# The product of state and C in two selective scans, moved to VectorE with C read from PSUM

## The chip, the cores and the metric

The kernel runs on one core of a Trainium2 chip. The metric is the device time of one execution in microseconds (us). Five engines work from queues of their own, each in order, and wait for one another by semaphores: TensorE (PE; its weight loads are shown as PEld), VectorE (DVE), ScalarE (ACT), GpSimd (POOL) and SyncE (SP), which here only issues DMAs.

## What is computed

The program is a decoder of four layers with three blocks each, on 16 sequences of 128 positions and 256 features. Two of the twelve blocks are selective state-space scans: the attention slot of layer 1 (512 inner channels) and that of layer 3 (256 channels). The change touches these two alone. The one of layer 3, cut to its core:

```python
A = jnp.exp(A_log)
Bm = h @ w_B.T + b_B                      # 16 states per position
Cm = h @ w_C.T + b_C
Delta = jax.nn.softplus((h @ w_d1.T + b_d1) @ w_d2.T + b_d2)
A_bar = jnp.exp(-Delta[..., None] * A)
BX = (Delta * h)[..., None] * Bm[:, :, None, :]
_, states = jax.lax.associative_scan(comb, (A_bar, BX), axis=1)
y = jnp.einsum('blfn,bln->blf', states, Cm) + D * h
```

The block of layer 1 computes the same recurrence from other projections.

## The kernel before

The twelve blocks run one after the other as stages, with a barrier of all engines between them. Channels lie on the 128 partitions, positions along the free dimension. The 16 sequences are taken in four groups of four, so a group has 4 x 128 = 512 columns (GT).

Both scan blocks share the class `Scan`. It works in units: one unit is a group and 256 channels, two slabs of 128, hence tiles of 128 x 2 x 512. The mamba stage (layer 1, 512 channels) has eight units, the sequence_ssm stage (layer 3) has four; I number them from 0 in each stage. A unit has 16 steps, one for each state n, 192 steps in all. A step n consists of

- "spread" n. TensorE multiplies a selecting matrix with the rows of B and C (L1156), which copies row n of B to all partitions in PSUM bank 4 and row n of C in bank 5. There are these two banks alone, so the spread of n+1 into a bank has to wait until the reader of n is done with it. ScalarE takes the exponentials into `decay` (L1173, two) and copies C's bank into the SBUF tile `ccol` (L1178). VectorE multiplies dt*x with B's bank into `drive` (L1188).
- "scan" n. VectorE runs the recurrence along the positions (L1196), from `decay` and `drive` into `state`. GpSimd then multiplies `state` in place with `ccol` (L1203).
- "sum" n. TensorE adds `state` to the unit's y in PSUM with an identity matrix (L1162): two matmuls in fp32, which the records show as four passes of 512 columns.

There are two tiles of decay, three of drive and three of state.

The order is written out by hand in `Scan.steps`. Every engine walks the same list and does its own part of each entry. Between the entries of a step stand two slots, a and b, each for one piece of other work: first what is left of the unit before ("finish", "out" and the like), then the preparation of the next group ("stats", "apply", "turn", "inner", "conv", "project", "split", "delta", "step" and others). A step reads: spread n+1, slot a, scan n, sum n-2, slot b. When a unit's pieces are used up, its steps are clean: only scan work is in them. At the end of a unit come sums 14 and 15, and behind them spread 0 of the next unit.

`Fills` counts how often a set of PSUM banks has been filled and emptied; its last argument names the engine that empties each bank in turn ("va": bank B by VectorE, bank C by ScalarE). The pieces that both stages put into the slots use two more banks, `side`.

## Time and profile before

| | us |
|---|---|
| median of 3 runs | 5046.37 |
| lowest, highest | 5042.47, 5047.23 |
| the profiled execution | 5043.2 |
| its span, first to last instruction | 5041.9 |

| engine | busy us | share of the span |
|---|---|---|
| TensorE | 3389.6 | 67% |
| VectorE | 2613.4 | 52% |
| ScalarE | 1957.9 | 39% |
| GpSimd | 1435.7 | 28% |

The shares are means over twelve stages that differ in what limits them, so they don't tell what the two scan stages wait for. In the timeline a row is one instruction or several merged ones of one engine and line; its columns are the start in us, the length in us, the engine, the line, the operation, the names written and read with their shapes, and how many instructions the row merges. In brackets stands the time for which the engine waited in front of it and what released it. An engine that starts an instruction before the record of the one ahead has ended shows starts closer together than the lengths; so steps are read from start to start. The granted clock of TensorE has two levels, full (2.4 GHz, 1.0) and half (1.2 GHz, 0.5), and a stretch shows its mean.

### The profile page before, as it was taken

How to read it: one execution, taken by the hardware profiler on the slowest of the kernel's cores; microseconds unless marked ns; L12 is line 12 of the kernel's file. 1: busy time of each engine (PE TensorE's matmuls, PEld its weight loads, DVE VectorE, ACT ScalarE, POOL GpSimd, SP SyncE). 2: the span in 40 equal slices, each digit the busy share in tenths (PEclk: the TensorE clock that was granted, in tenths of full speed). 3: DMA queues.
4: the chain of work that ended last, by engine and by line, in shares of the span. 5: the costliest groups of instructions: out<-in, count | busy, mean ns of one | idle time of the engine just before them, and what ended most of it. 6: DMA issues, size and time to landing. Idle time of an engine off the chain costs nothing. (4 is left out here: it accounts for less than half of the span.)

```text
span 5041.9 us, 52801 instructions
## 1 busy us (share of the span) xinstructions
PE 3389.6 (67%) x17501; PEld 2163.4 (43%) x17501; DVE 2613.4 (52%) x6543; ACT 1957.9 (39%) x3879; POOL 1435.7 (28%) x1085
## 2 busy tenths in 40 slices
PE   2666666638695366666668888856759766666688
PEld 1445544535463122222246656634546522224555
DVE  3555555534633488778933323354543257674443
ACT  2777777721121343443323333322412243433411
POOL 1444444421144334334411111120001134440010
PEclk8888888868898678777889999978968878788889
DMA  3000000012044100000000000011021200000000
GB/s 78 1 1 1 1 1 1 1 46 100 20 126 119 64 0 0 0 0 0 0 13 7 1 1 1 1 33 69 1 84 35 51 21 0 0 0 24 1 1 17
DMA packets 70666, 116.10 MB, mean 23 GB/s; under 512 B 28321, under 2 KB 58169, under 8 KB 67650
## 3 DMA queue, kind: packets, MB, share of 16 engines
q1 hardware_dynamic: 60802, 86.49, 5.4%
q0 software_dynamic: 9600, 26.23, 2.1%
q8 instruction: 148, 2.42, 0.2%
q14 instruction: 116, 0.95, 0.1%
HBM read 88.58 MB, written 24.12 MB: 22 GB/s over the span
## 5 line engine op out<-in xcount | busy, mean ns | idle before, releaser
L1203 POOL TENSOR_TENSOR L_attn_state<-L_attn_state,L_attn_ccol 128x1024 f32<-128x1024 f32 x192 | 481.1, 2509 | 678.7 <-DVE L_attn_state L1196 678.7
L1196 DVE TENSOR_TENSOR_SCAN L_attn_state<-L_attn_decay,L_attn_drive 128x1024 f32<-128x1024 f32 x192 | 583.1, 3042 | 0.2
L1162 PE MATMUL bank<-L_attn_state,ident 128*128 128x512 f32 x768 | 476.7, 757 | 60.4 <-POOL L_attn_state L1203 60.4
L1173 ACT ACTIVATE L_attn_decay<-L_attn_dt,L_attn_A 128x512 f32<-128x512 f32 x384 | 256.3, 715 | 344.2 <-DVE L_attn_state L1196 342.6
L1156 PE MATMUL bank<-L_attn_parts,L_attn_select 96*128 96x512 bf16 x384 | 158.4, 454 | 292.5 <-DVE L_attn_drive L1188 160.8
L1162 PEld LDWEIGHTS bank<-L_attn_state,ident 128*128 128x128 f32 x768 | 181.8, 242 | 259.9 <-issue 159.6
L1188 DVE TENSOR_TENSOR L_attn_drive<-L_attn_dtx,bank 128x1024 f32<-128x1024 f32 x192 | 230.4, 1200 | 111.3 <-PE bank L1156 111.2
L1083 POOL TENSOR_TENSOR L_xattn_prob<-L_xattn_prob,L_xattn_inv 128x1024 f32<-128x1024 f32 x64 | 121.3, 1895 | 570.9 <-DVE L_xattn_inv L1066 570.9
L1156 PEld LDWEIGHTS bank<-L_attn_parts,L_attn_select 96*128 96x128 bf16 x384 | 37.1, 106 | 479.6 <-DVE L_attn_drive L1188 260.7
L1178 ACT COPY L_attn_ccol<-bank 128x512 f32<-128x512 f32 x192 | 112.2, 585 | 295.2 <-POOL L_attn_state L1203 179.5
L716 ACT ACTIVATE L_xattn_prob<-bank,L_xattn_top 128x128 f32<-128x128 f32 x512 | 135.8, 416 | 197.1 <-DVE L_xattn_top L758 197.1
L2729 POOL TENSOR_TENSOR L_attn_t<-L_attn_t 128x512 f32<-128x512 f32 x96 | 121.7, 1268 | 305.5 <-ACT L_attn_t L2542 305.4
L1007 ACT ACTIVATE L_xattn_prob<-L_xattn_masked,L_xattn_low 128x256 f32<-128x256 f32 x256 | 126.9, 496 | 210.0 <-DVE L_xattn_low L1061 121.9
L2725 POOL TENSOR_TENSOR L_attn_t<-L_attn_t,L_attn_base 128x1024 f32<-128x1024 f32 x96 | 183.2, 1908 | 62.1 <-DVE L_attn_base L2675 62.1
L2698 DVE RECIPROCAL L_attn_den<-L_attn_den 128x512 f32<-128x512 f32 x32 | 107.3, 3353 | 139.4 <-ACT L_attn_den L2580 139.4
L1061 DVE CUSTOM_DVE_ANT_0 L_xattn_masked<-bank,L_xattn_hidden 128x256 f32<-128x256 f32 x256 | 93.3, 421 | 130.9 <-PE bank L921 130.9
L898 PE MATMUL bank<-L_xattn_kvT,L_xattn_wk 128*128 128x256 f32 x512 | 127.6, 392 | 37.2 <-ACT L_xattn_kT L963 19.6
L2679 DVE MATCH_REPLACE8 L_attn_t<-L_attn_top,L_attn_t 128x64 f32<-128x64 f32 x768 | 150.3, 207 | 0.0
L907 PE MATMUL bank<-L_xattn_wv,L_xattn_kvT 128*128 128x512 f32 x256 | 127.0, 618 | 28.6 <-ACT L_xattn_v L971 16.7
L2491 PE MATMUL bank<-L_attn_sm,L_attn_fv 128*64 128x128 f32 x512 | 50.0, 357 | 122.1 <-issue 122.1
L3379 POOL DMA_INDIRECT L_ffn_xh<-L_ffn_rows,L_ffn_tokens x96 | 91.2, 950 | 136.5 <-PE bank L3186 77.4
L2440 PE MATMUL bank<-L_attn_kbd,L_attn_qT 128*128 128x512 f32 x192 | 125.3, 743 | 0.0
(605 smaller groups left out, 8271.0 us busy)
## 6 DMA issues: line engine op xcount, KB each, us to landing
L_ffn_ew<-in_L_ffn_experts SPq DMA_DIRECT2D x4, 3072.0 KB, 20.0
L_ffn_made<-L_ffn_yout SPq DMA_DIRECT2D x24, 512.0 KB, 3.0
L_ffn_w<-in_L_ffn_w SPq DMA_DIRECT2D x4, 2048.0 KB, 14.6
L_xattn_ctx<-in_ctx_rows SPq DMA_DIRECT2D x3, 2048.0 KB, 8.3
L_ffn_rows<-L_ffn_xh SPq DMA_DIRECT2D x8, 512.0 KB, 3.0
L_ffn_made<-L_ffn_yout SPq DMA_DIRECT2D x12, 256.0 KB, 2.1
X<-in_x SPq DMA_DIRECT2D x16, 128.0 KB
turned<-X SPq DMA_DIRECT2D x16, 128.0 KB
```

The costliest lines, as they stand in the source:

```text
L716: t = act.activation(prob[n % 2][j][:, i, :], score[j].bank(n)[:, i * P:(i + 1) * P], ACT.Exp, bias=top[:, j, i:i + 1])
L898: t = pe.matmul(side.bank(at)[:, i * 2 * P:(i + 1) * 2 * P], w["wk"][:, k, col:col + P], kvT[a % 2][:, k, :], start=k == 0, stop=k == KC - 1)
L907: t = pe.matmul(side.bank(at)[:, :], kvT[a % 2][:, k, half * P:(half + 1) * P], w["wv"][:, k, cols], start=k == 0, stop=k == KC - 1)
L1007: t = act.activation(prob[n % 3][:, h, :], masked[n % 2][:, h, :], ACT.Exp, bias=low[:, n % 2, h:h + 1], scale=-1.0, accum_out=total[:, n ...
L1156: pe.matmul(self.spread.bank(2 * N + i)[:, :], self.select[:, NSTATE * i + n, :], parts[:, :], start=True, stop=True).then_inc(*self.sprea ...
L1162: t = pe.matmul(self.y[unit % len(self.y)][m][:, :], self.c.ident[:, :], self.state[N % 3][:, m, :], start=n == 0, stop=n == 15)
L1173: t = act.activation(self.decay[N % 2][:, m, :], dt[:, m, :], ACT.Exp, scale=A[:, m, n:n + 1])
L1188: dve.tensor_tensor(self.drive[N % 3][:, :, :], dtx[:, :, :], self.spread.bank(2 * N)[:, :].unsqueeze(1).broadcast_to([P, 2, GT]), ALU.mul ...
L1196: dve.tensor_tensor_scan(flat(self.state[N % 3]), flat(self.decay[N % 2]), flat(self.drive[N % 3]), 0.0, ALU.mult, ALU.add).then_inc(*self ...
L1203: pool.tensor_tensor(state[:, :, :], state[:, :, :], self.ccol[N % 2][:, :].unsqueeze(1).broadcast_to([P, 2, GT]), ALU.mult).then_inc(*sel ...
L2679: m = dve.match_replace(t[n % RING][:, 1, i, :], top[n % 2][:, i, :], t[n % RING][:, 0, i, :], -1e30)
L2725: pool.tensor_tensor(both, both, base[n % 2][:, :].unsqueeze(1).unsqueeze(3).broadcast_to([P, 2, per, nkeys]), ALU.subtract).then_inc(*shi ...
```

## The change

ScalarE's copy of C (`ccol`) and GpSimd's product are taken out. VectorE does the product right behind the scan, in place on `state`, with the second operand read from C's PSUM bank. It first waits for C's spread and for its own scan, and its end marks C's bank as empty and the state as ready for the sum. In `steps` the spread of n+1 moves from ahead of slot a to behind the scan of n: a step now reads slot a, scan n, spread n+1, sum n-2, slot b.

```diff
-        self.spread = Fills(s, "spread", banks, "va")
+        self.spread = Fills(s, "spread", banks, "v")
...
         yield "spread", 16 * unit
         for n in range(16 * unit, 16 * unit + 16):
+            yield from one()
+            yield "scan", n
             if n % 16 != 15:
                 yield "spread", n + 1
-            yield from one()
-            yield "scan", n
             if n % 16 >= 2:
                 yield "sum", n - 2
             yield from one()
...
-            pe.wait_ge(*self.weighted.at(N))
+            pe.wait_ge(*self.spread.emptied(2 * N + 1))
...
-            if N >= 2:
-                act.wait_ge(*self.weighted.at(N - 2))
-            act.wait_ge(*self.spread.filled(2 * N + 1))
-            act.copy(self.ccol[N % 2][:, :], self.spread.bank(2 * N + 1)[:, :]).then_inc(*self.spread.done(2 * N + 1))
...
-    def gpsimd(self, what, N):
-        if what == "scan":
-            pool, state = self.c.nc.gpsimd, self.state[N % 3]
-            pool.wait_ge(*self.spread.emptied(2 * N + 1))
-            pool.wait_ge(*self.scanned.at(N))
-            pool.tensor_tensor(state[:, :, :], state[:, :, :], self.ccol[N % 2][:, :].unsqueeze(1).broadcast_to([P, 2, GT]), ALU.mult).then_inc(*self.weighted.up())
+            state = self.state[N % 3]
+            dve.wait_ge(*self.spread.filled(2 * N + 1))
+            dve.wait_ge(*self.scanned.at(N))
+            dve.tensor_tensor(state[:, :, :], state[:, :, :], self.spread.bank(2 * N + 1)[:, :].unsqueeze(1).broadcast_to([P, 2, GT]), ALU.mult).then_inc(*self.spread.done(2 * N + 1))
```

The rest of the diff drops `ccol`, the flag `weighted` and the calls of `scan.gpsimd`. Lines behind it move up by a few, so L1188 and L1196 of before are L1184 and L1192 after, the product is L1196 after, and the convolution of the sequence_ssm stage, L1546 before, is L1537.

VectorE in the sequence_ssm stage, unit 1, steps 5 to 7, before. Names are the tiles written and read; the scan is listed as SCALAR_TENSOR_TENSOR, L1655 is the piece "inner" and L1661 begins the piece "normal":

```order
L1196 SCALAR_TENSOR_TENSOR L_attn_state_35170<-L_attn_decay_35166,L_attn_drive_35167 128x1024
L1655 TENSOR_SCALAR L_attn_h_35139<-bank,L_attn_cols 128x4x128
L1188 TENSOR_TENSOR L_attn_drive_35169<-L_attn_dtx_35147,bank 128x1024
L1655 TENSOR_SCALAR L_attn_h_35139<-bank,L_attn_cols 128x4x128
L1196 SCALAR_TENSOR_TENSOR L_attn_state_35171<-L_attn_decay_35165,L_attn_drive_35168 128x1024
L1188 TENSOR_TENSOR L_attn_drive_35167<-L_attn_dtx_35147,bank 128x1024
L1196 SCALAR_TENSOR_TENSOR L_attn_state_35172<-L_attn_decay_35166,L_attn_drive_35169 128x1024
L1661 BN_STATS L_attn_cbn_35153<-bank 128x6 x4
```

And after, the same place:

```order
L1192 SCALAR_TENSOR_TENSOR L_attn_state_34786<-L_attn_decay_34782,L_attn_drive_34783 128x1024
L1196 TENSOR_TENSOR L_attn_state_34786<-L_attn_state_34786,bank 128x1024
L1184 TENSOR_TENSOR L_attn_drive_34784<-L_attn_dtx_34763,bank 128x1024
L1646 TENSOR_SCALAR L_attn_h_34755<-bank,L_attn_cols 128x4x128 x2
L1192 SCALAR_TENSOR_TENSOR L_attn_state_34787<-L_attn_decay_34781,L_attn_drive_34784 128x1024
L1196 TENSOR_TENSOR L_attn_state_34787<-L_attn_state_34787,bank 128x1024
L1184 TENSOR_TENSOR L_attn_drive_34785<-L_attn_dtx_34763,bank 128x1024
L1192 SCALAR_TENSOR_TENSOR L_attn_state_34788<-L_attn_decay_34782,L_attn_drive_34785 128x1024
L1196 TENSOR_TENSOR L_attn_state_34788<-L_attn_state_34788,bank 128x1024
L1184 TENSOR_TENSOR L_attn_drive_34783<-L_attn_dtx_34763,bank 128x1024
L1652 BN_STATS L_attn_cbn_34769<-bank 128x6 x4
```

Scan, product and drive now follow one another, a drive is the one for the very next scan, and the pieces of slot b and of the next slot a stand together.

TensorE at the same place before (L1533 is "turn", L1539 "inner", L1546 "conv"):

```order
L1533 MATMUL bank<-ident,L_attn_xn 128x128 x4
L1162 MATMUL bank<-L_attn_state_35171,ident 128x512 x2
L1539 MATMUL bank<-L_attn_xT,L_attn_w_in 128x512 x2
L1156 MATMUL bank<-L_attn_parts_35149,L_attn_select_35164 128x512 x2
L1539 MATMUL bank<-L_attn_xT,L_attn_w_in 128x512 x2
L1162 MATMUL bank<-L_attn_state_35172,ident 128x512 x2
L1546 MATMUL bank<-L_attn_h_35139,L_attn_w_conv 128x512 x6
L1156 MATMUL bank<-L_attn_parts_35149,L_attn_select_35164 128x512 x2
L1546 MATMUL bank<-L_attn_h_35139,L_attn_w_conv 128x512 x6
L1162 MATMUL bank<-L_attn_state_35170,ident 128x512 x2
```

And after:

```order
L1524 MATMUL bank<-ident,L_attn_xn 128x128 x8
L1156 MATMUL bank<-L_attn_parts_34765,L_attn_select_34780 128x512 x2
L1162 MATMUL bank<-L_attn_state_34787,ident 128x512 x2
L1530 MATMUL bank<-L_attn_xT,L_attn_w_in 128x512 x4
L1156 MATMUL bank<-L_attn_parts_34765,L_attn_select_34780 128x512 x2
L1162 MATMUL bank<-L_attn_state_34788,ident 128x512 x2
L1537 MATMUL bank<-L_attn_h_34755,L_attn_w_conv 128x512 x12
L1156 MATMUL bank<-L_attn_parts_34765,L_attn_select_34780 128x512 x2
L1162 MATMUL bank<-L_attn_state_34786,ident 128x512 x2
```

Spread and sum stand together in front of the two pieces, where a piece stood between them; the two convolutions are one block of twelve matmuls behind the spread.

## Rows read from the trace of the kernel before

**Rows 1.** Costliest groups: line, engine, names, count | busy us, mean ns | idle before.

```profile
L1203 POOL TENSOR_TENSOR L_attn_state<-L_attn_state,L_attn_ccol 128x1024 f32<-128x1024 f32 x192 | 481.1, 2509 | 678.7 <-DVE L_attn_state L1196 678.7
L1196 DVE TENSOR_TENSOR_SCAN L_attn_state<-L_attn_decay,L_attn_drive 128x1024 f32<-128x1024 f32 x192 | 583.1, 3042 | 0.2
```

**Rows 2.** Timeline of clean steps, mamba unit 3, all engines.

```profile
2079.43 2.28 DVE L1196 TENSOR_TENSOR_SCAN L_attn_state<-L_attn_decay,L_attn_drive 128x1024 f32<-128x1024 f32 x1
2081.64 1.20 DVE L1188 TENSOR_TENSOR L_attn_drive<-L_attn_dtx,bank 128x1024 f32<-128x1024 f32 x1
...
2081.86 2.35 POOL L1203 TENSOR_TENSOR L_attn_state<-L_attn_state,L_attn_ccol 128x1024 f32<-128x1024 f32 x1 [12.64 <-DVE L_attn_state L1196]
2082.75 3.61 DVE L1196 TENSOR_TENSOR_SCAN L_attn_state<-L_attn_decay,L_attn_drive 128x1024 f32<-128x1024 f32 x1
...
2086.28 1.19 DVE L1188 TENSOR_TENSOR L_attn_drive<-L_attn_dtx,bank 128x1024 f32<-128x1024 f32 x1
...
2087.40 3.61 DVE L1196 TENSOR_TENSOR_SCAN L_attn_state<-L_attn_decay,L_attn_drive 128x1024 f32<-128x1024 f32 x1
```

**Rows 3.** Timeline at the end of mamba unit 2, all engines.

```profile
2058.99 5.79 DVE L1196 TENSOR_TENSOR_SCAN L_attn_state<-L_attn_decay,L_attn_drive 128x1024 f32<-128x1024 f32 x2
...
2062.75 6.47 POOL L1203 TENSOR_TENSOR L_attn_state<-L_attn_state,L_attn_ccol 128x1024 f32<-128x1024 f32 x2 [2.29 <-DVE L_attn_state L1196]
...
2066.97 6.55 PE L1162 MATMUL bank<-L_attn_state,ident 128*128 128x512 f32 x8 [3.51 <-POOL L_attn_state L1203]
...
2073.88 1.22 DVE L1188 TENSOR_TENSOR L_attn_drive<-L_attn_dtx,bank 128x1024 f32<-128x1024 f32 x1 [9.09 <-PE bank L1156]
...
2076.79 1.40 DVE L1418 SCALAR_TENSOR_TENSOR L_attn_xc<-L_attn_xc,L_attn_cols,bank 128x512 f32<-128x512 f32 x2
```

**Rows 4.** Timeline, mamba unit 2, VectorE: scans 0, 8 and 12.

```profile
1947.73 2.28 DVE L1196 TENSOR_TENSOR_SCAN L_attn_state<-L_attn_decay,L_attn_drive 128x1024 f32<-128x1024 f32 x1
...
2010.68 2.28 DVE L1196 TENSOR_TENSOR_SCAN L_attn_state<-L_attn_decay,L_attn_drive 128x1024 f32<-128x1024 f32 x1
...
2051.02 2.29 DVE L1196 TENSOR_TENSOR_SCAN L_attn_state<-L_attn_decay,L_attn_drive 128x1024 f32<-128x1024 f32 x1
```

**Rows 5.** Timeline, sequence_ssm unit 1, VectorE: scans 0, 2, 3, 6, 8, 12, next 0.

```profile
4202.78 2.28 DVE L1196 TENSOR_TENSOR_SCAN L_attn_state<-L_attn_decay,L_attn_drive 128x1024 f32<-128x1024 f32 x1
...
4214.34 2.28 DVE L1196 TENSOR_TENSOR_SCAN L_attn_state<-L_attn_decay,L_attn_drive 128x1024 f32<-128x1024 f32 x1
...
4220.16 2.26 DVE L1196 TENSOR_TENSOR_SCAN L_attn_state<-L_attn_decay,L_attn_drive 128x1024 f32<-128x1024 f32 x1
...
4249.57 2.28 DVE L1196 TENSOR_TENSOR_SCAN L_attn_state<-L_attn_decay,L_attn_drive 128x1024 f32<-128x1024 f32 x1
...
4262.82 2.28 DVE L1196 TENSOR_TENSOR_SCAN L_attn_state<-L_attn_decay,L_attn_drive 128x1024 f32<-128x1024 f32 x1
...
4296.80 2.28 DVE L1196 TENSOR_TENSOR_SCAN L_attn_state<-L_attn_decay,L_attn_drive 128x1024 f32<-128x1024 f32 x1
...
4325.30 2.28 DVE L1196 TENSOR_TENSOR_SCAN L_attn_state<-L_attn_decay,L_attn_drive 128x1024 f32<-128x1024 f32 x1
```

**Rows 6.** Timeline, VectorE: an instruction that waits for the one before it.

```profile
1729.65 1.22 DVE L1404 TENSOR_TENSOR L_attn_dt<-L_attn_dt,L_attn_soft 128x1024 f32<-128x1024 f32 x1 [10.11 <-ACT L_attn_soft L1358]
1730.91 1.23 DVE L1407 TENSOR_TENSOR L_attn_dtx<-L_attn_dt,L_attn_xc 128x1024 f32<-128x1024 f32 x1
```

**Rows 7.** Timeline, sequence_ssm unit 1, steps 5 and 6, ScalarE and TensorE.

```profile
4238.42 0.59 ACT L1178 COPY L_attn_ccol<-bank 128x512 f32<-128x512 f32 x1 [5.05 <-POOL L_attn_state L1203]
...
4244.66 1.88 PE L1162 MATMUL bank<-L_attn_state,ident 128*128 128x512 f32 x4
...
4246.37 2.74 PE L1546 MATMUL bank<-L_attn_h,L_attn_w_conv 128*128 128x512 f32 x6
```

**Rows 8.** Busy time by window: us, each engine (count), granted clock, DMA share, GB/s.

```profile
4200.00:4325.00 125.00, 79.89 (x174) 32.95 (x174) 85.05 (x97) 52.40 (x78) 54.13 (x32) 0.80 0.00 0
```

**Rows 9.** One line's instructions: count, ns min/median/max, first and last start, forms.

```profile
L1390 DVE SCALAR_TENSOR_TENSOR L_attn_xc<-L_attn_xi,L_attn_cols,L_attn_xc x48: 750/752/2724, 1695.6 to 2223.7; 128x512 f32<-128x512 f32 x48
```

More of the change, by code:

```diff
@@ L1104, in __init__ @@
         self.decay, self.drive = [s.sb(f"decay{n}", [P, 2, GT]) for n in range(2)], [s.sb(f"drive{n}", [P, 2, GT]) for n in range(3)]
-        self.state, self.ccol = [s.sb(f"state{n}", [P, 2, GT]) for n in range(3)], [s.sb(f"ccol{n}", [P, GT]) for n in range(2)]
+        self.state = [s.sb(f"state{n}", [P, 2, GT]) for n in range(3)]
         self.mid, self.rest = s.sb("mid", [2 * NSTATE, GT], BF16), s.sb("rest", [2 * NSTATE, GT])
-        self.spread = Fills(s, "spread", banks, "va")
+        self.spread = Fills(s, "spread", banks, "v")
         self.y = [ybanks[2 * n:2 * n + 2] for n in range(len(ybanks) // 2)]
-        self.decayed, self.scanned, self.weighted, self.summed = (s.flag(n) for n in ("decayed", "scanned", "weighted", "summed"))
+        self.decayed, self.scanned, self.summed = (s.flag(n) for n in ("decayed", "scanned", "summed"))
         self.selected, self.split_up, self.parted = s.flag("selected"), s.flag("split_up", 4), s.flag("parted")
@@ L1455, in gpsimd @@
             pool.tensor_tensor(rs, rs, power[:, :], ALU.mult).then_inc(*norm.inverse.up())
-        elif what == "scan":
-            scan.gpsimd(what, n)
     return Part(order, tensor, scalar, vector, gpsimd)
@@ L1771, in gpsimd @@
             last.root(n)
-        elif what == "scan":
-            scan.gpsimd(what, n)
     return Part(order, tensor, scalar, vector, gpsimd)
```

## The prediction

> **What bounds the kernel now.** I read the list of costliest groups first. Its two top rows are a pair: GpSimd's product of state and C (L1203) and VectorE's scan (L1196), 192 of each [rows 1]. Both scan stages ("mamba" and "sequence_ssm") are VectorE's. The timeline of a stretch with no side work shows it [rows 2]: a scan starts at 2082.75, the next multiply into drive at 2086.28, the next scan at 2087.40, so a step is 4.65 us and VectorE never stops. The reader is to see one more thing there. The scan at 2079.43, which comes after a pause of GpSimd, takes 2.28; the later ones take 3.61, because GpSimd's product (2.35, started at 2081.86) still runs when they are due and holds them until it ends at 2084.21. So a clean step costs 1.11 + 2.20 (both start to start) and 1.33 of being held.
>
> Two other kinds of time lie in these stages. At the end of each unit of 16 steps VectorE waits for TensorE: GpSimd needs 6.47 us for the last two products, TensorE's last eight summing passes start only at 2066.97, the next unit's spread comes behind them, and drive starts at 2073.88, after 9.09 us of waiting [rows 3]; there are 12 such ends. And where the next group's preparation is woven in (units 0, 2, 4 of the first stage, all but the last of the second), VectorE often waits for a piece's matmuls. One unit of each stage stands in rows by its scans [rows 4, 5].
>
> **The change, part by part.** *GpSimd's product and ScalarE's copy go.* With no GpSimd work beside it a scan is 2.28 again, worth 1.33 in each of some 110 held ones (583.1 - 192 x 2.28 = 145 us, and 145 / 1.33 = 109) [rows 1, 2]. ScalarE's copy lies beside other work; nothing on VectorE waits for it in a clean step.
>
> *VectorE gets 192 products*, of 128x1024 with one PSUM operand, the form of drive (1.20) [rows 2]. The product reads what the scan just wrote, and now each drive stands right in front of its scan, so two starts a step wait for VectorE's own last result. Such a pair stands in [rows 6]: 1.22 long, next start after 1.26, so 0.04 after the end, where an unbound next one starts 0.08 before it (1.19 to 1.11). A clean step becomes 2.28 + 0.04, 1.22 - 0.08, 1.19 + 0.04 = 4.69 us: 0.04 longer than before. Bounds: 4.62 if the bound starts cost nothing, 4.85 if all three pay 0.1. The Trainium skill ("VectorE: DVE Perf Modes", the section on the TRN2 errata) gives a PSUM source 120 fixed cycles and an SBUF source 58, some 0.065 us more for each product; by it the sum would be 12 us higher. The rows speak against it: drive with a PSUM operand takes 1.20, the pair with two SBUF operands 1.22 and 1.23 [rows 6].
>
> *The unit's end.* Let T be the start of scan 15. Product 14 ended at T - 1.15. Behind it TensorE has C's spread, the sums 12, 13, 14, 15 (four passes each) and the next B's spread: about 18 passes. A pass is 0.43 at the full clock (a sum of four starts at 4244.66, the work behind it 1.71 later) and twice that, 0.86, at the half one [rows 7]; with a granted clock of 0.80 over a unit, 0.6 of the time is full and a mean pass is 0.54 [rows 8]. So drive 16 starts at T - 1.1 + 18 x 0.54 = T + 8.6 (T + 6.7 all full, T + 13.7 all half); before it was T + 11.3 (scans 14 and 15 take 5.79 from 2058.99, so T is 2062.53). Then drive 1.14 and finish 2.64 (two L1418, one L1422, read from 2076.79 to 2079.43): 12.4 from scan to scan, against 16.9. A clean unit is thus 15 x 4.69 + 12.4 = 82.8 where 83.0 stood: nothing. The gain at the end pays for a drive that used to be done before the unit began.
>
> *The spread on TensorE, the part that decides.* C(n+1) goes into the bank that C(n) leaves, and TensorE's queue is in order. Before, ScalarE's copy emptied that bank early, so TensorE ran ahead: at 4244.66 it did a sum and from 4246.37 the first conv passes, while the scan on VectorE only began at 4249.57 [rows 5, 7]. Now that bank is free only at P, the end of product n. Queued behind this wait are C(n+1), sum n-2, the piece of slot b and the piece of the next slot a; ScalarE's copies and VectorE's own pieces wait for these. TensorE reaches slot b at P + 0.1 + 0.45 + 2.15 = P + 2.7, VectorE is there at P + 1.15. The order also joins slots b and a, with scan, product and drive all on the other side.
>
> I walk the sequence unit from 4202.78 to 4325.30 [rows 5], scan to scan, now and then:
> - scans 0 to 2 (back, last, out): 11.6, then 15.0. back starts after product 0 (3.45) instead of beside scan 0.
> - 2 to 3 (out, stats): 5.8, then 11.2: 3.45 + 2.7 + 2.5 passes' time of out, 0.95 for its add, 1.7 for stats.
> - 3 to 6 (whole, apply, turn, inner): 29.4, then 26.8. ScalarE's copy of C, held 5.05 us by GpSimd at 4238.42 with the copy of xT behind it, is gone [rows 7].
> - 6 to 8 (conv, normal, [rows 7]): 13.3, then 21.6: 3.45 + 2.7, both convs as one block of 24 passes at the full clock 10.4, spread 0.4, and then drive 1.15 and twice 1.7 of normal. Scan 7 and its product hide in it.
> - 8 to 12 (silu, project, rank, split, delta, step): 34.0, then 43.5. project starts 1.6 later, rank and delta each start 2.7 behind a product, and the chain through ScalarE starts that much later.
> - 12 to the next unit: 28.5, then 3 x 4.69 + 12.4 = 26.5.
>
> Sum 122.5, then 144.6: +22. The next unit is the same at 120.9 (+24), the first has no finish pieces (+13), the last has them and nothing more, and ends a little sooner (+9): +68 for this stage.
>
> The same walk for the mamba unit from 1947.73 to 2079.43 [rows 2, 4]: scans 0 to 8 (out, stats, apply, four convs that are VectorE's own) 62.9, then 66.8, all of it in the out and apply pieces; 8 to 12 (silu, project, delta, split, step) 40.3, then 47.6, of which project and delta, held as above, are 3.5 and 3.8; the rest 28.4, then 26.5. Sum 131.7, then 140.9: +9. Unit 4 is the same work in 129.0, +12. Unit 0, where stats and apply now have scan, product and drive between them, -1; the five others together 0. First stage: +20.
>
> **Sum.** The profiled execution took 5043.2 (span 5041.9 and 1.3 around it), 3.2 below the median of 5046.4. 5043.2 + 20 + 68 = 5131; against the median I forecast **5134 us**. The unknown that moves it most is TensorE's pass: all mixed segments at 0.43 would give about 35 us back, all at 0.86 would add about 50.
>
> **Rivals.**
> - *The products hide, chance 0.09, 5010 us (faster).* Of the 125 us around the unit of [rows 5] VectorE is busy 85 [rows 8], so some 30 us of waits lie in its mixed steps. If every product there falls into a wait that some other chain sets (GpSimd's root, ScalarE's tables), the mixed segments keep their times. Then eight mixed units gain 2 us each (end less tail), and the pieces that GpSimd holds behind a scan get shorter: eight of the 48 of L1390 from 2.72 to 0.75 [rows 9], 16 us, with some 4 of others: -36. For it: the stretch 3 to 6 above, where ScalarE's queue was the cause. Against it: TensorE's in-order wait on the product, which lengthens just the chains that VectorE waits for. It decides if TensorE gets to slot b less than 1.15 after P. Near it stands the Trainium skill ("SBUF — State Buffer", "Who interferes with whom"): of a VectorE instruction with two SBUF inputs and a GpSimd one that reads SBUF, the second is blocked whole; by that rule the 145 us of held scans come back.
> - *Halves of both, chance 0.05, 5046:* full clock throughout the mixed segments and half of their products hidden.
> - *TensorE mostly at its half clock in the held segments, chance 0.10, 5184:* it now stands still before each block, and eight passes after a pause took 6.55 us [rows 3], nearly all at the half clock.
> - *The hold isn't GpSimd's, chance 0.03, 5280:* if 3.61 stays, 110 steps of 6.0 add 150 us. Against it: the one scan of 2.28 [rows 2], with the same operands, and GpSimd's end at 2084.21 plus 2.2 is the scan's end.
>
> **How the numbers follow.** Forecast 0.73 with 5090 to 5175 as its own range. The range of 8 in 10 goes from 5075 to 5182. A measurement of this kernel tells about 0.2% (10 us) from no change. Slower by more: 0.73 + 0.10 + 0.03 and a little of the mixed case, 0.87; within: 0.04; faster: 0.09.
>
> **What would show it.** Right: scans all near 2.28; clean steps at 4.65 to 4.75; idle of VectorE before drive or before normal of about 9 us at the convs of the sequence stage, released by TensorE; TensorE's spread released by VectorE's product, with the sum and the piece starting behind it; drive of a new unit 8 to 9 us after scan 15 starts. Wrong: convs of the sequence stage starting before product 6 ends, unchanged segments 6 to 8 and 8 to 12, or clean steps off 4.69 by more than 0.1, each tenth of which is worth 11 us.

## The result, and the profile after

| | before | after |
|---|---|---|
| median of 4 runs, us | 5046.8 | 5411.06 |
| lowest, highest | 5042.47, 5049.84 | 5406.45, 5415.06 |
| span of the profiled execution | 5041.9 | 5407.8 |
| ratio, 95% interval | | 1.0722, 1.0704 to 1.0741 |

The change makes the kernel slower by 364 us. The forecast was slower by 88, in a range that ended at 5182. The direction was right and the size was wrong by a factor of four.

The scan's row among the costliest groups after, in the columns of [rows 1]:

```profile
L1192 DVE TENSOR_TENSOR_SCAN L_attn_state<-L_attn_decay,L_attn_drive 128x1024 f32<-128x1024 f32 x192 | 439.3, 2288 | 315.2 <-PE bank L1162 313.6
```

The scan was busy 583.1 us in [rows 1] and is busy 439.3 now: the 144 us in which GpSimd held it are back, as forecast. But in front of it stand 315 us of idle time, where the row of before had 0.2, and nearly all of that ended with TensorE's sum (L1162). VectorE's waits, listed by what ended them (us in total, times, longest), say it once more:

```profile
DVE L_attn_state L1192 <- PE bank L1162: 313.6, 118, 3.0
```

118 waits of at most 3.0 us are some 2.7 us each. The timeline of clean steps shows one of them (mamba unit 3, VectorE and TensorE; before: [rows 2]):

```profile
2197.98 2.29 DVE L1192 TENSOR_TENSOR_SCAN L_attn_state<-L_attn_decay,L_attn_drive 128x1024 f32<-128x1024 f32 x1 [2.98 <-PE bank L1162]
...
2200.38 1.22 DVE L1196 TENSOR_TENSOR L_attn_state<-L_attn_state,bank 128x1024 f32<-128x1024 f32 x1
2201.52 1.21 DVE L1184 TENSOR_TENSOR L_attn_drive<-L_attn_dtx,bank 128x1024 f32<-128x1024 f32 x1
...
2201.66 0.61 PE L1156 MATMUL bank<-L_attn_parts,L_attn_select 96*128 96x512 bf16 x1 [3.29 <-DVE L_attn_state L1196]
...
2202.06 3.62 PE L1162 MATMUL bank<-L_attn_state,ident 128*128 128x512 f32 x4
...
2205.47 0.63 PE L1156 MATMUL bank<-L_attn_parts,L_attn_select 96*128 96x512 bf16 x1
2205.72 2.29 DVE L1192 TENSOR_TENSOR_SCAN L_attn_state<-L_attn_decay,L_attn_drive 128x1024 f32<-128x1024 f32 x1 [2.99 <-PE bank L1162]
```

The reader is to follow a circle. The product ends at 2201.60. C's spread starts at 2201.66, when its bank is free, and the sum follows it at 2202.06. The sum ends at 2205.68 (2202.06 + 3.62), and the next scan starts at 2205.72. Then come scan and product, and it begins anew: 7.73 us a step, of which VectorE is busy 4.64. The scan waits for this sum because there are only three tiles of state: scan n writes the tile that sum n-3 reads (`summed.at(N - 3)`), and the sum that stands behind C(n) is sum n-3. The four passes take 3.62 at the half clock; elsewhere in the same unit a sum takes less and a step 7.0 to 7.5. Steps 0 and 1 of a clean unit take 4.88, since no sum stands behind their spreads yet. Of the 364 us, 212 lie in the first stage and 149 in the second (from its first scan to that of the second, and from there to the end of the program).

The windows of one clean unit and one with pieces (length; busy and count of PE, PEld, DVE, ACT, POOL; granted clock, DMA share, GB/s) show both stages: 83.0 us became 116.9 and 122.5 became 159.4, and the clock fell from 0.79 in both units to 0.68 and 0.70.

```profile
2143.76:2260.62 116.86, 62.29 (x96) 20.99 (x96) 76.84 (x52) 21.34 (x32) 0.00 (x0) 0.68 0.00 0
4449.12:4608.51 159.39, 91.32 (x174) 36.89 (x174) 94.46 (x110) 40.54 (x60) 13.00 (x16) 0.70 0.00 0
```

### The profile page after: what moved, and what is told of

It is laid out like the page before. It is cut to its first block and busy times, and to the rows that moved or that the text cites. A ratio compares the mean times of both kernels' runs of the same rounds, so it can differ in the third digit from the quotient of the medians.

```text
span 5407.8 us, 52415 instructions
## 1 busy us (share of the span) xinstructions
PE 3493.5 (65%) x17501; PEld 2201.0 (41%) x17501; DVE 2680.1 (50%) x6735; ACT 1839.4 (34%) x3681; POOL 953.8 (18%) x893
## 5 line engine op out<-in xcount | busy, mean ns | idle before, releaser
L1156 PE MATMUL bank<-L_attn_parts,L_attn_select 96*128 96x512 bf16 x384 | 194.5, 515 | 724.6 <-DVE L_attn_state L1196 678.0
L1192 DVE TENSOR_TENSOR_SCAN L_attn_state<-L_attn_decay,L_attn_drive 128x1024 f32<-128x1024 f32 x192 | 439.3, 2288 | 315.2 <-PE bank L1162 313.6
L1162 PE MATMUL bank<-L_attn_state,ident 128*128 128x512 f32 x768 | 574.6, 900 | 0.7 <-DVE L_attn_state L1196 0.6
L1162 PEld LDWEIGHTS bank<-L_attn_state,ident 128*128 128x128 f32 x768 | 217.6, 284 | 202.9 <-issue 183.7
L1184 DVE TENSOR_TENSOR L_attn_drive<-L_attn_dtx,bank 128x1024 f32<-128x1024 f32 x192 | 233.2, 1215 | 51.5 <-PE bank L1156 50.9
L1196 DVE TENSOR_TENSOR L_attn_state<-L_attn_state,bank 128x1024 f32<-128x1024 f32 x192 | 234.5, 1222 | 20.0
L639 PE MATMUL bank<-ident,L_xattn_prob 128*128 128x128 f32 x512 | 87.6, 312 | 55.6 <-ACT L_xattn_pT L694 55.6
```

Source lines behind the costliest of these rows:

```text
L1156: pe.matmul(self.spread.bank(2 * N + i)[:, :], self.select[:, NSTATE * i + n, :], parts[:, :], start=True, stop=True).then_inc(*self.sprea ...
L1162: t = pe.matmul(self.y[unit % len(self.y)][m][:, :], self.c.ident[:, :], self.state[N % 3][:, m, :], start=n == 0, stop=n == 15)
L1184: dve.tensor_tensor(self.drive[N % 3][:, :, :], dtx[:, :, :], self.spread.bank(2 * N)[:, :].unsqueeze(1).broadcast_to([P, 2, GT]), ALU.mul ...
L1192: dve.tensor_tensor_scan(flat(self.state[N % 3]), flat(self.decay[N % 2]), flat(self.drive[N % 3]), 0.0, ALU.mult, ALU.add).then_inc(*self ...
L1196: dve.tensor_tensor(state[:, :, :], state[:, :, :], self.spread.bank(2 * N + 1)[:, :].unsqueeze(1).broadcast_to([P, 2, GT]), ALU.mult).the ...
```

## The experiments

Theory A is the circle read above. Against it stand: B, the product on VectorE costs the time by itself; C, the pieces that are held behind C's spread cost it, which was the prediction's own mechanism; D, TensorE's low clock costs it, whoever waits. The kernel before ran beside each kernel at a median of 5044 to 5053 us.

### A fourth tile of state

```diff
-            if N >= 3:
-                dve.wait_ge(*self.summed.at(N - 3))
+            if N >= 4:
+                dve.wait_ge(*self.summed.at(N - 4))
```

and `state` has four tiles, taken by N % 4.

> The changed kernel with a fourth state tile; scan n then waits for sum n-4 instead of sum n-3. Nothing else differs. Theory A (a loop: the end of product n-1 frees C's bank, C(n) and behind it sum n-3 run on TensorE, and scan n waits for that sum because there are three state tiles): the wait goes, steps without a piece take 4.7 to 4.9 us instead of 7.1 to 7.7, and with some 110 such steps at 2.6 us each the time is 5110 to 5160 us. Theory B (VectorE's product and its own waits cost that much): steps and time stay, 5411 us. Theory C (only the pieces held behind C's spread cost time): the clean steps stay, 5411 us. Theory D (TensorE at its half clock is the cause by itself, whoever waits): steps stay above 7 us.

Measured 5145.66 us, 1.020 of before (1.0183 to 1.0217). The clean steps, timeline of mamba unit 3, VectorE and TensorE:

```profile
2127.01 1.22 DVE L1196 TENSOR_TENSOR L_attn_state<-L_attn_state,bank 128x1024 f32<-128x1024 f32 x1
2128.15 1.21 DVE L1184 TENSOR_TENSOR L_attn_drive<-L_attn_dtx,bank 128x1024 f32<-128x1024 f32 x1
2128.29 0.39 PE L1156 MATMUL bank<-L_attn_parts,L_attn_select 96*128 96x512 bf16 x1 [1.40 <-DVE L_attn_state L1196]
...
2128.51 1.88 PE L1162 MATMUL bank<-L_attn_state,ident 128*128 128x512 f32 x4
...
2129.49 2.29 DVE L1192 TENSOR_TENSOR_SCAN L_attn_state<-L_attn_decay,L_attn_drive 128x1024 f32<-128x1024 f32 x1
```

The sum still starts right behind C's spread, but the scan starts at 2129.49 while it runs (to 2130.39) and waits for nothing but its own drive. A step is 4.88 us. It stays so when the sum is slow: in an earlier step of this unit the four passes take 3.62, as long as in the kernel after, and the next scan still comes 4.88 behind the one before it.

```profile
2099.06 3.62 PE L1162 MATMUL bank<-L_attn_state,ident 128*128 128x512 f32 x4
...
2099.87 2.29 DVE L1192 TENSOR_TENSOR_SCAN L_attn_state<-L_attn_decay,L_attn_drive 128x1024 f32<-128x1024 f32 x1
...
2104.75 2.29 DVE L1192 TENSOR_TENSOR_SCAN L_attn_state<-L_attn_decay,L_attn_drive 128x1024 f32<-128x1024 f32 x1
```

One tile takes 265 of the 364 us away, so A holds, and B and D can't carry that part: the product is still there, and so are slow sums. What remains is within 12 us of the forecast of 5134, which was in effect a forecast of this kernel: its two stages were forecast 20 and 68 us longer than before and are 24 and 80 longer here.

### The sum ahead of the spread

```diff
             yield "scan", n
-            if n % 16 != 15:
-                yield "spread", n + 1
             if n % 16 >= 2:
                 yield "sum", n - 2
+            if n % 16 != 15:
+                yield "spread", n + 1
```

> The changed kernel with the sum n-2 listed ahead of the spread of n+1 behind scan n, three state tiles. Sum n-2 then runs before TensorE waits for product n, so scan n+1 no longer stands behind product n's end plus a sum. Theory A: steps without a piece 4.7 to 4.9 us, the time 5110 to 5170 us, like the kernel with four state tiles. Theories B, C and D: steps of 7.1 to 7.7 and 5411 us as before.

Measured 5081.43 us, 1.0075 (1.0058 to 1.0091), and clean steps of 4.88. This breaks the circle at another place with three tiles, and it is better than expected: 64 us below the fourth tile. The sequence unit of [rows 5] took 122.5 before, 149.7 with four tiles and 133.8 here. With the sum ahead of the waiting spread, it no longer stands between product n and the piece behind it. That is theory C's mechanism, with the sum as one more thing in the queue.

### Both at once

The two edits above together.

> Both cures of the loop at once: the changed kernel with four state tiles and with sum n-2 ahead of the spread of n+1. The fourth tile alone gave 5146 us and the sum first alone 5081. If the fourth tile does nothing but break the loop, it adds nothing where the sum is first: 5070 to 5090 us, steps without a piece 4.88. If the scan in the steps with pieces also waits for sums of three steps back, another 10 us or more goes: under 5070.

Measured 5087.96 us (5077.41 to 5091.98), the same ratio as with the sum first alone (1.0073 and 1.0075). The unit of [rows 5] takes 133.8 in both. So the fourth tile does nothing else than break the circle.

### Half of the sum

```diff
-            for m in range(2):
+            for m in range(1):
                 t = pe.matmul(self.y[unit % len(self.y)][m][:, :], self.c.ident[:, :], self.state[N % 3][:, m, :], start=n == 0, stop=n == 15)
```

> The changed kernel with one of the two matmuls of each sum left out, so that y of the first slab alone is computed. Theory A: the loop is shorter by two passes, 1.7 us at the half clock, so steps without a piece take 5.5 to 6.0 us and the time falls by some 190 us or more, to 5150 to 5230 us. Theories B and C: TensorE's sums are hidden, steps of 7.1 to 7.7 stay and the time is within 20 us of 5411 us.

Measured 5234.06 us, clean steps of 6.03. Two rows, the sum of a clean step and the scan it releases:

```profile
2161.26 1.91 PE L1162 MATMUL bank<-L_attn_state,ident 128*128 128x512 f32 x2
...
2163.21 2.29 DVE L1192 TENSOR_TENSOR_SCAN L_attn_state<-L_attn_decay,L_attn_drive 128x1024 f32<-128x1024 f32 x1 [1.28 <-PE bank L1162]
```

7.73 - 6.03 = 1.70, and the sum went from 3.62 to 1.91, two passes less at the half clock: the step follows the length of the sum one to one. Both values lie just outside of what was expected (at most 6.0 and 5230). TensorE did less and was granted less: the clock of the clean unit is 0.54, after 0.68 with the whole sum. So the passes that are left are nearly all at the half clock.

### More work for TensorE

```diff
                 for gone in self.spread.before(2 * N + i):
                     pe.wait_ge(*gone)
+                for _ in range(6 if i == 0 and n >= 2 else 0):
+                    pe.matmul(self.spread.bank(2 * N)[:, :], self.select[:, n, :], parts[:, :], start=True, stop=True)
                 pe.matmul(
```

> The changed kernel with six more matmuls on TensorE in each step from the third of a unit on: B's spread is written six times more into its own bank before it is announced, in the 3.3 us in which TensorE stands and waits for the product. It computes the same. Theory A together with the clock (the loop is as long as it is because the sum's four passes run at the half clock): if the added work lifts the granted clock, a sum takes 1.7 instead of 3.4 to 3.6 us, steps 5.7 to 6.1 instead of 7.1 to 7.7, and the time is 5180 to 5260 us although more is computed. If the clock isn't the price, or isn't lifted: 5411 to 5450 us.

Measured 5316.01 us, so 95 us less than after with 1008 matmuls more. The direction is that of the theory, the size isn't: 5180 to 5260 was expected. The timeline of mamba unit 3, one step after the other, shows why:

```profile
2150.77 3.27 PE L1164 MATMUL bank<-L_attn_state,ident 128*128 128x512 f32 x4
...
2154.08 2.29 DVE L1194 TENSOR_TENSOR_SCAN L_attn_state<-L_attn_decay,L_attn_drive 128x1024 f32<-128x1024 f32 x1 [2.64 <-PE bank L1164]
...
2157.98 1.88 PE L1164 MATMUL bank<-L_attn_state,ident 128*128 128x512 f32 x4
...
2159.90 2.29 DVE L1194 TENSOR_TENSOR_SCAN L_attn_state<-L_attn_decay,L_attn_drive 128x1024 f32<-128x1024 f32 x1 [1.07 <-PE bank L1164]
```

From the scan at 2154.08 to that at 2159.90 are 5.82, with a sum at the full clock; the step before it took 7.39, with a sum of 3.27. Four of this unit's 13 steps with a sum are as short as that, the others between 7.3 and 7.7, at a mean clock of 0.80. So the low clock is a part of the circle's price (some 1.6 us a step where it is gone), but it isn't what makes it: with a fourth tile there are sums of 3.62 too, and nobody waits for them.

### The order alone

The kernel before, with only the entries of a step in the new order (slot a, scan n, spread n+1, sum n-2, slot b):

```diff
         for n in range(16 * unit, 16 * unit + 16):
+            yield from one()
+            yield "scan", n
             if n % 16 != 15:
                 yield "spread", n + 1
-            yield from one()
-            yield "scan", n
```

> The kernel before with the new order of a step alone (slot a, scan n, spread n+1, sum n-2, slot b); the product stays on GpSimd and ScalarE still copies C. If the order costs by itself, by joining two slots and putting drive right in front of its scan, VectorE's waits in the steps with pieces grow and the time is 5070 to 5110 us; if what costs is only that C's bank is freed by the product, the time is 5035 to 5060 us, since ScalarE's copy still frees the bank early.

Measured 4992.77 us, 0.9893 (0.9876 to 0.9909). Neither expectation holds: the order isn't neutral, it gains 52 us. Two places give it. The first is the end of a unit: from scan 15 to the next unit's scan 0 it took 15.5 to 17.0 us before and takes 12.1 to 13.8 here. The timeline at the end of mamba unit 3, rows of VectorE, GpSimd and TensorE (before, [rows 3] show the like at the end of unit 2):

```profile
2128.91 2.35 POOL L1203 TENSOR_TENSOR L_attn_state<-L_attn_state,L_attn_ccol 128x1024 f32<-128x1024 f32 x1 [2.29 <-DVE L_attn_state L1196]
2130.01 3.40 DVE L1196 TENSOR_TENSOR_SCAN L_attn_state<-L_attn_decay,L_attn_drive 128x1024 f32<-128x1024 f32 x1
2131.32 1.98 PE L1162 MATMUL bank<-L_attn_state,ident 128*128 128x512 f32 x4 [1.99 <-POOL L_attn_state L1203]
2133.55 2.34 POOL L1203 TENSOR_TENSOR L_attn_state<-L_attn_state,L_attn_ccol 128x1024 f32<-128x1024 f32 x1 [2.29 <-DVE L_attn_state L1196]
2135.95 1.98 PE L1162 MATMUL bank<-L_attn_state,ident 128*128 128x512 f32 x4 [2.64 <-POOL L_attn_state L1203]
...
2138.28 1.22 DVE L1188 TENSOR_TENSOR L_attn_drive<-L_attn_dtx,bank 128x1024 f32<-128x1024 f32 x1 [4.87 <-PE bank L1156]
```

The drive for scan 15 now stands between scans 14 and 15, so product 14 starts during it and sum 14 is done before scan 15 ends. In [rows 3] both scans ran back to back, the two products followed as one block of 6.47, and eight passes stood behind it. VectorE waited 9.09 there and waits 4.87 here. A part of this is paid ahead of scan 15, since the step from 14 to 15 now holds a drive: 4.65 for 3.53. From scan 14 to the next scan 0 the ten ends between units give 22 us together. The other place is larger: the six units with pieces of the next group are 32 us shorter up to scan 14. In the unit of [rows 5] it is the stretch from scan 3 to scan 6, 29.4 before and 23.4 here.

### The product alone

The kernel before with its own order and with ScalarE's copy of C, but the product on VectorE, from that copy in SBUF:

```diff
-    def gpsimd(self, what, N):
-        if what == "scan":
-            pool, state = self.c.nc.gpsimd, self.state[N % 3]
-            pool.wait_ge(*self.spread.emptied(2 * N + 1))
-            pool.wait_ge(*self.scanned.at(N))
-            pool.tensor_tensor(
+            state = self.state[N % 3]
+            dve.wait_ge(*self.spread.emptied(2 * N + 1))
+            dve.wait_ge(*self.scanned.at(N))
+            dve.tensor_tensor(
```

> The kernel before with its own order and ScalarE's copy of C, but with the product on VectorE, read from that copy in SBUF: the move alone, without the bank that the product holds. Held pieces theory: with C's bank free early TensorE runs ahead as before, the steps with pieces take what they took or less, a clean step is 4.88 us (scan, product and drive with three starts that wait for VectorE's own last result, as with four state tiles), the units end in 10 us instead of 17, and the time is 4980 to 5030 us. Rival, the product costs its 1.22 us in the steps with pieces too, held or not: 5070 to 5110 us.

Measured 4987.19 us, 0.9892 (0.9876 to 0.9909), within the first range. B has fallen: 192 products on VectorE cost nothing net, and gain 57 us, when TensorE may run ahead. The clean step is 4.66, not the 4.88 that was expected: drive stands ahead of the scan before, so only the product's start waits for VectorE's own last result. The step was 4.65 before, so the product takes the place of the 1.33 us for which the scan was held. The gain lies at the ends: 11.6 us from scan 15 to the next scan in all but one (10 was expected), and 44 us less over the ten ends, from scan 14 on. The unit of [rows 5] takes 114.7 where it took 122.5.

### C's spread apart

One edit on the sum-first kernel: C's spread is its own entry, right ahead of its scan.

```diff
             yield from one()
+            yield "spread_c", n
             yield "scan", n
             if n % 16 >= 2:
                 yield "sum", n - 2
             if n % 16 != 15:
                 yield "spread", n + 1
             yield from one()
```

> The kernel with the sum first (5081 us) with one edit more: C's spread of n is taken out of the pair and stands right ahead of scan n, behind slot a; B's spread, decay and drive stay where the change put them, behind scan n. Its difference to the sum-first kernel is only that sum and pieces no longer stand on TensorE behind a spread that waits for the product. If held pieces are what is left of the loss, the time is 4975 to 5000 us and the sequence stage's unit 1 takes 113 to 118 us instead of 133.8. If B's place made the difference between 5081 and 4983, it stays at 5060 to 5085 us.

Measured 4997.61 us, 0.9892 (0.9876 to 0.9909): 84 us less than the sum-first kernel, and the unit of [rows 5] goes from 133.8 to 115.6. C was right as a mechanism, at 84 us. The convolutions of the sequence stage show it; first the sum-first kernel, then this one, TensorE and VectorE:

```profile
4254.72 2.28 DVE L1192 TENSOR_TENSOR_SCAN L_attn_state<-L_attn_decay,L_attn_drive 128x1024 f32<-128x1024 f32 x1
...
4258.38 0.61 PE L1156 MATMUL bank<-L_attn_parts,L_attn_select 96*128 96x512 bf16 x1 [3.51 <-DVE L_attn_state L1196]
...
4258.78 13.15 PE L1537 MATMUL bank<-L_attn_h,L_attn_w_conv 128*128 128x512 f32 x24
```

```profile
4198.71 2.28 DVE L1197 TENSOR_TENSOR_SCAN L_attn_state<-L_attn_decay,L_attn_drive 128x1024 f32<-128x1024 f32 x1
...
4198.92 10.46 PE L1542 MATMUL bank<-L_attn_h,L_attn_w_conv 128*128 128x512 f32 x24
```

Above, the block starts 4.06 us after scan 6, behind the product, and TensorE, which stood still for 3.51, needs 13.15 for it. Below it starts 0.21 after the scan and takes 10.46. VectorE's waits for B's spread ahead of drive fall from 79.6 us in 25 to 29.0 in 14:

```profile
DVE L_attn_drive L1184 <- PE bank L1156: 79.6, 25, 10.8
```

```profile
DVE L_attn_drive L1189 <- PE bank L1157: 29.0, 14, 2.8
```

The same with B's spread, decay and drive of n+1 back ahead of slot a, as the kernel before had them:

> The changed kernel, three state tiles, product from PSUM, with B's spread of n+1 back ahead of slot a and C's spread of n as an entry of its own right ahead of scan n. Now no piece stands on TensorE between C's spread and the product that it waits for: both pieces and the sum run during scan and product. Against the kernel with the sum first (5081 us; the sequence stage's unit 1 took 133.8 us, the first stage's unit 2 took 137.5): held pieces theory, these two units go to 110 to 120 and 125 to 131 us and the time to 4980 to 5030 us. Rival, what is left over the kernel before is VectorE's product itself: 5070 to 5090 us.

Measured 4983.24 us, 0.9878 (0.9861 to 0.9894). The two units took 115.8, as expected, and 121.0, less than the 125 to 131 expected. B's place is thus worth 14 us at the most. A clean step is 4.66 here and 4.88 with B's spread behind the scan, but the end of a unit is 11.6 to 13.3 us against 9.8 to 10.2.

### The next unit's first spread early

```diff
-        yield "spread", 16 * unit
+        if unit == 0:
+            yield "spread", 0
         for n in range(16 * unit, 16 * unit + 16):
-            if n % 16 != 15:
+            if n + 1 < 16 * self.units:
                 yield "spread", n + 1
-            yield from one()
+            if n % 16:
+                yield from one()
             yield "spread_c", n
```

> As the kernel with C's spread apart, and besides the next unit's first spread of B, its decay and its drive stand ahead of scan 15 of the unit that ends, and the first slot of a unit stays empty, so that the finishing piece comes behind scan 0. If the end of a unit waits for TensorE's last sums with B's spread behind them, scan 15 to the next scan falls from some 10 us to 6 or less plus 2.6 for finish in the next step, 2 to 4 us for each of 10 ends: 15 to 40 us below the kernel with C's spread apart. Rival, the waits go to scan 0's or scan 1's step in full: within 10 us of it.

Measured 4979.26 us (4977.57 to 4984.31). The rival holds: 4 us less than the kernel with C's spread apart and B's ahead of slot a (4983). Scan 15 to the next scan did fall from 11.6 to 13.3 us to 7.1 to 7.7, but the work that had to be there by then came with it: clean units went from 80.3 to 82.0 only to 79.7.

### The product one scan behind

On the kernel with the early first spread: scan n, then product n-1; C's spread of n-1 ahead of scan n, and the finishing pieces two steps into the unit.

```diff
-            yield "spread_c", n
+            if n:
+                yield "spread_c", n - 1
             yield "scan", n
+            if n:
+                yield "product", n - 1
...
-            state = self.state[N % 3]
-            dve.wait_ge(*self.filled_c.at(N))
+        elif what == "product":
+            state = self.state[N % 3]
+            dve.wait_ge(*self.filled_c.at(N))
```

> The kernel with C's spread apart and the early first spread of a unit (4979 us), with the product of n-1 as an entry of its own behind scan n; the finishing pieces start two steps into a unit, behind the last sum. In a clean step of the changed kernel three starts wait for VectorE's own last result (0.08 us of idle each, 4.88 in all). Here scan, product and drive each use what was done one instruction earlier or more. If the idle time is those waits, a clean step is 2.20 + 1.14 + 1.11 = 4.45 us, a clean unit 72 to 75 instead of 79.7, and the time 4915 to 4950 us. Rival, the idle time is the engine's own cost of a wait on any semaphore: steps stay at 4.8 and the time within 15 us of 4979.

Measured 4932.17 us (4926.91 to 4932.74), 0.977 of before (0.9754 to 0.9787): the best kernel of the study, 2.3% faster than before. Its clean steps, VectorE alone:

```profile
2083.85 2.28 DVE L1207 TENSOR_TENSOR_SCAN L_attn_state<-L_attn_decay,L_attn_drive 128x1024 f32<-128x1024 f32 x1
2086.05 1.19 DVE L1212 TENSOR_TENSOR L_attn_state<-L_attn_state,bank 128x1024 f32<-128x1024 f32 x1
...
2087.17 1.21 DVE L1199 TENSOR_TENSOR L_attn_drive<-L_attn_dtx,bank 128x1024 f32<-128x1024 f32 x1
...
2088.30 2.28 DVE L1207 TENSOR_TENSOR_SCAN L_attn_state<-L_attn_decay,L_attn_drive 128x1024 f32<-128x1024 f32 x1
```

A step is 2.20 + 1.12 + 1.13 = 4.45, and a clean unit takes 74.0 us, of which VectorE is busy 73.7; 83.0 stood before. The kernel that this one was made from has the product right behind its scan:

```profile
2085.28 2.28 DVE L1199 TENSOR_TENSOR_SCAN L_attn_state<-L_attn_decay,L_attn_drive 128x1024 f32<-128x1024 f32 x1
2087.67 1.22 DVE L1203 TENSOR_TENSOR L_attn_state<-L_attn_state,bank 128x1024 f32<-128x1024 f32 x1
2088.81 1.21 DVE L1191 TENSOR_TENSOR L_attn_drive<-L_attn_dtx,bank 128x1024 f32<-128x1024 f32 x1
2089.94 2.29 DVE L1199 TENSOR_TENSOR_SCAN L_attn_state<-L_attn_decay,L_attn_drive 128x1024 f32<-128x1024 f32 x1
```

Its starts are 2.39 (scan to product), 1.14 and 1.13 apart, 4.66 in all: one start waits for VectorE's own last result. In the fourth-tile kernel above they are 2.40, 1.14 and 1.34, since there the scan comes right behind its drive too. So 4.88, 4.66 and 4.45 are the clean steps with two, one and no such start. The expectation counted three of them and took 4.88 for the step of the kernel it started from; the drive behind the product was never bound.

## Why the prediction was right and wrong

By medians, the 364 us are made up along a chain of kernels: the order alone -54 (5046.8 to 4992.8), three edits at once, the product to VectorE with PSUM, the sum first and C's spread apart, +5 (to 4997.6), C's spread back beside B's, with pieces held behind it +84 (to 5081.4), the sum behind that spread +330 (to 5411.1). The kernel before, measured beside each of them, has medians up to 9 us apart, so the first two terms are known to about that.

- **The step that failed** is in "The spread on TensorE, the part that decides". It names what is queued behind C's spread: "C(n+1), sum n-2, the piece of slot b and the piece of the next slot a; ScalarE's copies and VectorE's own pieces wait for these". The list was right, and the sum stood in it. Who waits for the sum was left out: scan n+1, through its wait for sum n-2 (three steps back, three tiles). Before, that sum had long been done, and no row showed the wait. It stood in the code, in the first line of the scan. The price was 118 waits and 313.6 us; the fourth tile takes 265 us off, and putting the sum ahead of the spread 330. The prediction's own times would have shown a good half of it: TensorE done with the sum at P + 2.7, VectorE ready at P + 1.15, so 1.55 us a wait, or 183 us over 118 waits, as an estimate. The waits were 2.7 us, because the four passes took 3.1 to 3.6 us in a clean unit and not 2.15: the sum used the clock of 0.80 from before [rows 8], and it fell to 0.68 to 0.70.
- **The clean step**, forecast at 4.69 with 4.85 as its upper bound, took 7.0 to 7.7, and 4.88 once the circle was broken. The two starts bound to VectorE's own last result were priced at 0.04 us after the end by [rows 6]. They cost 0.11 (2.40 - 2.29) and 0.13 (1.34 - 1.21). With lengths that are 0.01 to 0.02 longer the step is 0.19 above the forecast, some 20 us over 110 steps. The upper bound of 4.85 was added up wrong: 0.1 at all three starts is 2.38 + 1.32 + 1.29 = 4.99, and 4.88 lies below that. The clean unit, forecast at 82.8, took 85.4 with four tiles and 83.7 with the sum first.
- **The held scans** came back as forecast: 583.1 to 439.3 is 144 us for 145, and no scan takes more than 2.3. The rival that the hold wasn't GpSimd's is out.
- **The price of a PSUM source.** The product's median is 1.222 us from PSUM, and 1.225 from ScalarE's copy in the kernel with the product alone. The Trainium skill ("VectorE: DVE Perf Modes", the section on the TRN2 errata) gives a PSUM source 120 fixed cycles and an SBUF source 58. The 0.065 us more that the prediction worked out from this doesn't show in these records, and the choice of the rows was right.
- **The unit's end** was forecast at 12.4 us from scan to scan and took 9.8 to 10.3. The walk put sums 12 to 15 and two spreads, 18 passes, behind product 14, and they do stand there: at the end of mamba unit 2 they fill the 10.2 us from product 14 to drive 16, where 9.7 were forecast. But the circle made scan 15 wait for sum 12, so it started 4.1 us behind product 14 and not 1.15. The time is no gain: it was lost in the step before. With four tiles, where the scan doesn't wait, five of the ten ends took 11.9 and the others 10.2. The bound for the half clock was mis-added: 18 x 0.86 gives T + 14.4, not T + 13.7.
- **The walk of the sequence unit** was right in its mechanism and mostly in size. Forecast and measured, in the order of its segments: 15.0 and 15.05; 11.2 and 12.6; 26.8 and 28.5; 21.6 and 23.1; 43.5 and 47.8; 26.5 and 32.4. With four tiles the second, third and last of them take 11.5, 27.1 and 24.8, so their surplus is mostly the circle's. 6 to 8 and 8 to 12 stay at 23.2 and 47.9: there the held chain was forecast 1.6 and 4.4 us too short, and which part of it was not taken apart. The sum over the unit is 149.7 with four tiles, for 144.6.
- **The rival "the products hide", 5010 us,** failed here by its condition, TensorE at slot b less than 1.15 us after the product. Where TensorE isn't held, the product costs nothing net, and the kernels that do this run at 4983 to 4998. In the clean steps it doesn't fall into a wait, though, but takes the place of the held time.
- **What the order does** was given no term. The walk charged it with joining slots. Alone it gains 52 us. The product's move alone, in the old order, gains 57. Together they give no more than one of them (4983 to 4998). The traces say where. Over the ten ends, from scan 14 to the next scan 0, the order takes off 22 us, the product's move 44, and both with C's spread apart 49: the same ends are shortened twice. Over the rest of the units, up to scan 14, the order takes off 31, the product's move 2, and both together add 11. A part of that is the clean step of 4.88, with drive right in front of its scan; why the rest of the order's gain doesn't come back was not tested.

A mixed term stays open: how the 330 us divide. 265 are the scan's wait. Another 64 go when the sum leaves the space between spread and piece, seen as 149.7 to 133.8 in the sequence unit and 143.8 to 137.5 in the mamba unit. The clock has a share in both: the kernel with more work for TensorE shows some 1.6 us a step, but only in some steps. How large that share is stays open.

## What to carry to other kernels

When a wait is added to an in-order queue, list everything behind it, and for each item everyone who waits for it, the buffer waits of the writers ("may I overwrite this tile?") too. Such a wait has no row as long as it is met early, so it must be read from the code: count the tiles and see whether the new order closes a circle through them. If it does, moving the reader ahead of the new wait is better than a further tile: it cost no memory here and was 64 us faster.

A resource that is freed late should be asked for late. C's spread, asked for just ahead of the scan, made the product wait four times, 12.4 us in all (kernel with C's spread apart); asked for a step early, it held TensorE's whole queue, at 84 us more.

## What the runs showed of the hardware

- A VectorE instruction that waits for the result of the one just ahead of it started 0.11 us (product behind scan) and 0.13 us (scan behind drive) after the end of it in the records; where the result that it waits for lay further back, it started 0.08 before the end of the one ahead. Drive moved ahead of the scan before took the clean step from 4.88 to 4.66, and the product moved behind the next scan from 4.66 to 4.45. The pair of [rows 6] had shown 0.04, so this price isn't the same for all pairs.
- TensorE's granted clock fell when work was taken away from it and rose when work was added. In clean mamba unit 3 it was 0.68 after, 0.54 with half of the sum left out, 0.80 with six matmuls more a step, and 0.79 before. More matmuls made the kernel 95 us faster.
- The operand's place decides whether GpSimd can hold the product. Read from SBUF, in the kernel with the product alone, three of the products took some 3.3 us instead of 1.23. The one behind scan 4 of the sequence unit lies beside a GpSimd addition of other data and ends 1.07 behind it (4190.49 and 4189.42), as if most of it had been done only then (timeline):

```profile
4187.06 2.36 POOL L1759 TENSOR_TENSOR X<-X,L_attn_b_out 128x1024 f32<-128x1024 f32 x1 [3.69 <-ACT X L1580]
4187.17 3.32 DVE L1201 TENSOR_TENSOR L_attn_state<-L_attn_state,L_attn_ccol 128x1024 f32<-128x1024 f32 x1
```

  In the kernel after, the product beside the same addition, started 0.12 us behind it (0.11 above), is read from PSUM and takes 1.22:

```profile
4312.38 2.36 POOL L1754 TENSOR_TENSOR X<-X,L_attn_b_out 128x1024 f32<-128x1024 f32 x1 [3.68 <-ACT X L1575]
4312.50 1.22 DVE L1196 TENSOR_TENSOR L_attn_state<-L_attn_state,bank 128x1024 f32<-128x1024 f32 x1
```

  All 192 took 1.22 there (the line's instructions: count, then ns shortest, median, longest; first SBUF, then PSUM):

```profile
L1201 DVE TENSOR_TENSOR L_attn_state<-L_attn_state,L_attn_ccol x192: 1224/1225/3327, 1740.7 to 4464.2; 128x1024 f32<-128x1024 f32 x192
```

```profile
L1196 DVE TENSOR_TENSOR L_attn_state<-L_attn_state,bank x192: 1220/1222/1223, 1749.7 to 4888.9; 128x1024 f32<-128x1024 f32 x192
```

  The drives of before, which read B from PSUM, say the same: 140 of the 192 overlap GpSimd work, and none takes more than 1.223. The hold also goes the other way. In the kernel with the product alone a GpSimd operation on 128x4 (L1438) that starts at 1738.61, 0.23 behind a scan, takes 2.02 and ends with the scan; beside a drive, at 1954.36, it takes 0.20.
